# Encoder of a vision tower on one core: the last softmax pair is normalised on VectorE, the last value gather runs on ScalarE, a reciprocal and some transpositions are moved

## The reference, cut to what matters

```python
for l in range(6):
    keys = concat([zeros, x])                      # one zero key ahead of the 37 tokens
    q, k, v = x @ Wq.T + bq, keys @ Wk.T + bk, keys @ Wv.T + bv     # 16 heads of 16
    attn = softmax(where(valid, q k^T / 4, -inf))  # over 38 keys
    o = (attn @ v) @ Wo[l].T + bo[l]
    x = LN(x + o) * ln1_g[l] + ln1_b[l]
    ff = gelu(x @ W1[l].T + b1[l]) @ W2[l].T + b2[l]
    x = LN(x + ff) * ln2_g[l] + ln2_b[l]
```

## Time and profile before

| what | value |
|---|---|
| median of 3 runs | 843.77 us (841.07 to 846.59) |
| span of the profiled execution | 838.5 us |
| encoder phases in it | from about 325 to about 778 us |
| PE busy | 786.8 us, 94% |
| DVE, ACT, POOL busy | 638.9, 458.5, 257.7 us |
| lone phase, PE | 325.1 to 354.0 us |
| a phase A, a phase B | about 36.2 us, about 35.1 us |

### The profile page before, as it was taken

One profiled execution on the slowest core, in us unless ns is written; L12 is line 12 of the kernel. 1 busy time (PEld: TensorE's weight loads), 2 busy tenths in 40 slices (PEclk: granted clock), 3 DMA queues, 4 the chain that ended last, 5 costly groups with the idle time before them and its releaser, 6 DMA issues.

```text
span 838.5 us, 15975 instructions
## 1 busy us (share of the span) xinstructions
PE 786.8 (94%) x5736; PEld 727.0 (87%) x5736; DVE 638.9 (76%) x1285; ACT 458.5 (55%) x820; POOL 257.7 (31%) x297
## 2 busy tenths in 40 slices
PE   5889899999999999799999999999999999979698
PEld 4788669999999998699989989998998999968466
DVE  5696493888877876778797887878788787875686
ACT  3386313433333336576676777677677767735421
POOL 0002100311111100364365146336525524723232
PEclk9899799999999999899999999999999999999999
DMA  5000935989898822010210021021011002200001
GB/s 185 1 1 1 379 105 200 335 298 346 306 336 317 332 75 105 0 40 14 79 61 0 16 97 38 13 100 38 13 50 54 33 13 100 81 23 1 0 1 30
DMA packets 18288, 88.33 MB, mean 105 GB/s; under 512 B 3120, under 2 KB 7472, under 8 KB 12240
## 3 DMA queue, kind: packets, MB, share of 16 engines
q1 hardware_dynamic: 18256, 87.90, 29.5%
HBM read 85.05 MB, written 2.84 MB: 105 GB/s over the span
## 4 chain that ended last, share of the span: by engine, by line
PE 47%; issue 22%; POOL 16%; DVE 11%; ACT 3%; DMA 1%; POOLq 0%; SPq 0%; DVEq 0%; ACTq 0%
PE bank L1093 14%; PE bank L1130 5%; POOL W_L L1925 5%; POOL HF_L L1979 4%; POOL arena L1911 4%; PE bank L1235 3%; POOL WQKV_L L1925 2%; PE bank L1139 2%; PE bank L724 2%; PE bank L866 2%; PE bank L849 2%; PE bank L781 2%; DVE OB L2091 2%; PE bank L766 2%; PE bank L1425 2%
## 5 line engine op out<-in xcount | busy, mean ns | idle before, releaser
L1093 PE MATMUL bank<-arena 128*128 (+1 forms) x1024 | 118.0, 274 | 0.5 <-ACT arena L1669 0.5
L1093 PEld LDWEIGHTS bank<-arena 128*128 128x128 f32 x1024 | 117.4, 192 | 0.7 <-ACT arena L1669 0.7
L1911 POOL TENSOR_TENSOR arena<-arena,srec 111x456 f32<-111x456 f32 x56 | 52.3, 962 | 128.3 <-DVE srec L2079 128.3
L1925 POOL TENSOR_TENSOR W_L<-LW,W_H 128x256 fp32r<-128x256 f32 x96 | 71.0, 778 | 29.5 <-DVE XHL L2520 25.8
L1979 POOL TENSOR_TENSOR HF_L<-arena,HF_H 128x296 fp32r<-128x296 f32 x48 | 43.8, 936 | 86.4 <-ACT HF_H L1826 86.4
L766 PE MATMUL bank<-XHL,W_H 128*128 128x296 f32 x288 | 66.3, 308 | 1.2 <-DVE arena L2068 1.2
L1826 ACT ACTIVATE arena<-bank,vec 128x296 f32<-128x296 f32 x96 | 48.8, 509 | 25.8 <-PE bank L766 17.9
L1937 POOL TENSOR_TENSOR QW<-QW,arena x14 | 22.4, 1599 | 119.0 <-DVE QW L2421 65.6
L1279 PE MATMUL bank<-HF_L,W_H 128*128 128x296 f32 x192 | 57.4, 299 | 0.0
L1279 PE MATMUL bank<-HF_H,W_H 128*128 128x296 f32 x192 | 57.4, 299 | 0.0
L1279 PE MATMUL bank<-HF_H,W_L 128*128 128x296 f32 x192 | 57.4, 299 | 0.0
(11 more groups left out here) (268 smaller groups left out, 2175.6 us busy)
## 6 DMA issues: line engine op xcount, KB each, us to landing
arena<-ew_in SPq DMA_DIRECT2D x16, 2048.0 KB, 8.9
arena<-ew_in SPq DMA_DIRECT2D x16, 1024.0 KB, 6.3
LW<-lw_in SPq DMA_DIRECT2D x12, 1024.0 KB, 4.9
arena<-route SPq DMA_DIRECT2D x32, 185.0 KB, 3.4
LW<-lw_in SPq DMA_DIRECT2D x6, 768.0 KB, 4.3
fp_weights<-arena SPq DMA_DIRECT2D x1, 2048.0 KB, 6.4
arena<-fp_weights SPq DMA_DIRECT2D x1, 2048.0 KB, 7.2
arena<-patches_in SPq DMA_DIRECT2D x2, 864.0 KB, 7.7
```

Of the source, the lines that this page charges most:

```text
L1093: last = mm(o[:, m * CAP:(m + 1) * CAP], w[:, kc, mi * P:(mi + 1) * P], xg(kc, e), start=(kc == 0), stop=(kc == C - 1))
L1911: nc.gpsimd.tensor_tensor(v, v, srec[0:QROWS, s:s + 2, :].unsqueeze(3).to_broadcast([QROWS, 2, C * JH, KEYS]), ALU.mult).then_inc(p_ready, 1)
L1925: last = nc.gpsimd.tensor_tensor(low[:, cols], value[:, cols], high[:, cols], ALU.subtract)
```

## The change

Four things are done in the encoder:

1. **Normalisation.** POOL normalises three pairs of a phase instead of four (`POOL_PAIRS = 3`). DVE multiplies the fourth pair itself (`normalise_last`), in phases A and B between the two residual additions of L2672, in the lone phase after its last reciprocal.
2. **Gather.** DVE gathers three chunks of four (`DVE_GROUPS = 3`). ACT gathers the last (`gather_last`), behind `ln_root` and ahead of `high_weights` and `high_stream`. In the third chunk DVE now takes the reciprocal of the deviation between the second and the third copy. `project_out` waits for DVE's third chunk ahead of its first products and for ACT's chunk ahead of those on feature chunk 1. A copy of the value bias (`vbias`) is made in `set_kbias`.
3. **Transpositions.** In phases A and B, the first of the four jobs of `turn_v` goes ahead of `ln_var_of`.
4. **Lone phase.** Pairs are interleaved: maximum, shift, sum and reciprocal of the early pairs come before those of the late ones on DVE, the exponent of pair 3 comes behind `probs_out` of pair 0 on ACT, and PE transposes two pairs, computes their values, then transposes the other two and computes theirs.

```diff
@@ phase_order
-    att("t", 0, 1, 2, 3)
-    att("o", 0, 1, 2, 3)
+    if y is None:
+        for g in range(2):
+            att("t", 2 * g, 2 * g + 1)
+            att("o", 2 * g, 2 * g + 1)
+    else:
+        att("t", 0, 1, 2, 3)
+        att("o", 0, 1, 2, 3)
@@ TensorE
+                if x and y:
+                    turn_v(rx, plan, hx, (0,))
                 if y:
                     ln_var_of((ly, 0), hy, ones_d)
...
-                    turn_v(rx, plan, hx)
+                    turn_v(rx, plan, hx, (1, 2, 3) if y else range(4))
...
+                elif x:
+                    for g in range(2):
+                        for i in range(2):
+                            transpose_probs(rx, plan, p0 + 2 * g + i)
+                        values(rx, plan, 2 * hx + g)
@@ ScalarE
+            def gather_last(r, plan, h):
+                c = C - 1
+                act.wait_ge(filled["o"], nth("o", 4 * h + 3, r))
+                o = bank_of(plan, ("o", 4 * h + 3))
+                def take(s, lo, hi):
+                    dst = images(OB[lo:hi, h, c, :])[:, 4:8, :]
+                    src = o[lo:hi, 0:4 * QROWS].rearrange("p (b s q) -> p b s q", b=4, s=JH)[:, :, s, :]
+                    return f(dst, src, ACT.Identity, bias=vbias[lo:hi, c:c + 1])
+                take(1, 0, 96).then_inc(o_lead_act, 1)
+                take(2, 96, P)
+                act.wait_ge(o_lead_act, once_a_phase(h, r))
+                take(0, 0, 48).then_inc(o_ready_act, 1)
...
                 if y:
                     ln_square((ly, 1), hy)
                     ln_root((ly, 1), hy)
+                if x:
+                    gather_last(rx, plan, hx)
                 if x:
                     if late_split(x) and late_split(x)[0] == "w1":
                         high_weights(*late_split(x))
@@ ScalarE, lone phase
+                    for i in range(3):
+                        exponent(rx, p0 + i)
+                    probs_out(rx, plan, p0)
+                    exponent(rx, p0 + 3)
+                    for i in range(1, HB // 2):
+                        probs_out(rx, plan, p0 + i)
+                    high_stream(1, 2)
@@ GpSimd
-                    normalise((x[1] * 2 + (x[0] + 2)) * (HB // 2), HB // 2)
+                    normalise((x[1] * 2 + (x[0] + 2)) * (HB // 2), POOL_PAIRS)
@@ VectorE
+            def normalise_last(r, h):
+                p = HB // 2 * (h + 1) - 1
+                dve.wait_ge(s_rec, nth("s", p, r))
+                v.tensor_tensor(pair_probs(p), pair_probs(p), pair_view(srec, p).unsqueeze(2).to_broadcast(
+                    [QROWS, 2 * C * JH, KEYS]), ALU.mult).then_inc(p_ready_dve, 1)
...
                         v.scalar_tensor_tensor(R[:, hy, c, :], bank_of(plan, ("f2", 2 * hy + c))[:, 0:NHALF],
                                                resid[:, ly, C + c:C + c + 1], XD[:, hy, c, :], ALU.add, ALU.add
                                                ).then_inc(ffn_added, 1)
+                        if x and c == 0:
+                            normalise_last(rx, hx)
...
-                if x and y:
-                    gather_values(rx, plan, 2 * hx + 1, lambda c: lv(lx, "bqkv", 2 * C + c), (0,))
-                if y:
+                if x:
+                    gather_values(rx, plan, 2 * hx + 1, lambda c: lv(lx, "bqkv", 2 * C + c), (0,),
+                                  (lambda: ln_recip((ly, 1), hy)) if y else None)
+                else:
                     ln_recip((ly, 1), hy)
-                if x:
-                    gather_values(rx, plan, 2 * hx + 1, lambda c: lv(lx, "bqkv", 2 * C + c),
-                                  (1,) if y else range(C))
```

91 lines of the change are left out of this document (64 added, 27 removed).

## The result

The changed kernel takes 851.01 us (849.49 to 853.56, 6 runs) against 843.12 for the kernel before (841.07 to 846.59, 6 runs) in the same job: ratio 1.0098, interval 1.007 to 1.0125. Measured once more (e13), it takes 849.18 us against 842.91, ratio 1.0072, interval 1.0049 to 1.0095. The change makes the kernel some 6 to 8 us slower; the forecast was 1.75.

The account below looks back on a forecast made before the run. PE, busy 94% of the span, was taken to bound the kernel. Terms 0 + 1.35 - 2.2 - 1.1 - 1.8 + 5.5 = +1.75 us on the 838.5 span gave 840.2, plus 5.3 to the median: 845.5, range 838 to 851.

Parts of the forecast that it names:

- The ScalarE queue behind the gather: Phases B: `gather_last` ahead of `W1_H` makes `XH` late by 1.1 us for the next phase; cost 5.5 in five phases.
- Normalising on DVE: Tail of each phase: DVE multiplies pair 3, so L707 comes 0.1 us earlier; gain 1.1 in eleven phases.
- The reciprocal inside the third chunk: Value gather: the reciprocal ends earlier and L733's wait goes; 0.3 us a phase, gain 1.8 in six phases A.
- The transposition ahead of the variance: Head of each phase: one `turn_v` job fills PE's 0.22 us wait before L724; gain 2.2 in ten phases.
- The lone phase: First transposition 2.0 us sooner, values ending where they did, clock falling as before; taken as 0, bounds 3 gained, 2.5 lost.
- half clock in the whole lone phase: Rival: values cost 0.21 us a record to the end of the lone phase; +2.5, 848.0 us; chance 0.10.
- The first A: First phase A: high weights behind ScalarE's gather delay `values_out`, squares and L724; cost 1.35 us, bounds 0.9 and 2.1.
- order free: Rival: ScalarE's order costs nothing, L781 shows no wait on `XH` in phases B; 834.0 us; chance 0.15.
- port costs more: Rival: `normalise_last` is held by POOL's pair 2 or holds it in full; 848.0 us, up to 853.5; chance 0.17.
- nothing: Rival: PE's waits only change owner and ACT's work is covered; 843.8 us; chance 0.10.

Follow-up runs that it names:

- e13: The changed kernel measured and profiled again, nothing edited: 849.18 us against 842.91 for the kernel before, ratio 1.0072.
- e6: The changed kernel with GpSimd (POOL) normalising all four pairs again, everything else as changed: 852.63 us, ratio 1.0109 to the kernel before.
- e4: The changed kernel with all four `turn_v` jobs back behind the variance: 853.61 us, ratio 1.011 to the kernel before.
- e8: Changed kernel with edits of e2 and e3, lone high weights ahead of ScalarE's gather, second half of keys ahead of root, VectorE order matched: 844.95 us, ratio 1.0043.
- e5: The changed kernel with 29 idle products (17, 6 and 6) added on TensorE in the lone phase: 845.63 us, ratio 1.004 to the kernel before.
- e12: e10 with `high_stream` ahead of `gather_last`, and in the lone phase two chunks gathered before `low_stream(1, 2)` and `W1_H` before ScalarE's gather: 851.58 us, ratio 1.0118.
- e2: The changed kernel with the lone phase in the old order, VectorE's normalisation and ScalarE's gather kept: 849.45 us, ratio 1.0064 to the kernel before.
- e3: The changed kernel with `high_stream` ahead of the high part of W1 on ScalarE in phases B, behind the gather: 844.80 us, ratio 1.0005 to the kernel before.
- e1: The kernel before plus the change's copy of the value bias and three unused semaphores, none of its orders: 842.78 us, ratio 0.9997.
- e9: The kernel before with idle products in its lone phase (17 ahead of the first transposition, 3 and 3 behind pairs): 847.05 us, ratio 1.0062.
- e10: e5 with 8 and 42 more idle products at two places behind the encoder: 843.82 us, ratio 1.0022 to the kernel before.
- e15: The kernel before with the 8 and 42 idle products of e10 behind its encoder, nothing else: 843.64 us, ratio 1.0001.
- e14: e12 with `high_stream` between ScalarE's gather and the weights, as in e3: 837.25 us against 842.91 for the kernel before, ratio 0.9919.

## Why the prediction was wrong, point by point

**The ScalarE queue behind the gather (+5.5): right.** The wait of L802 on `XH` of about 1 us, five times, was forecast (4.9 in 5). The phases B lose 0.9 each against a forecast of 0.78. A term was undersized: the gather cost 0.379 per copy (`Identity` with a bias from SBUF) and not the 0.286 that I took from L1570 in the earlier trace rows, so 1.18 in all instead of 0.87.

```profile
L1625 ACT ACTIVATE OB<-bank,vbias x36: 377/379/381, 358.9 to 757.8; 96x148 f32<-96x148 f32 x12, 32x148 f32<-32x148 f32 x12, 48x148 f32<-48x148 f32 x12
```

**Normalising on DVE (-1.1): right in the sum, wrong in a reading.** Forecast 0.1 a phase, measured 0.12 to 0.13 (e6). The multiplication took 0.74, not 0.63, and `RSUM` was in time, as forecast. POOL's three pairs take 3.17, which is 0.4 more than three of the 0.92 each in the earlier trace rows; the forecast was 0.42. All of it is in the third:

```profile
424.32 1.34 POOL L1974 TENSOR_TENSOR arena<-arena,srec 111x456 f32<-111x456 f32 x1
```

The prediction held it against the skill's rule that POOL's block had grown by only 0.26, less than VectorE's whole instruction. But an instruction can lose only what is left of the other when it is issued. The third pair starts at 424.32, VectorE's multiplication ends at 424.85, so 0.53 was left, and the pair grew by 0.39. On the other side, in the kernel before, `RSUM` started at 416.63 with 0.79 left of a POOL pair and grew by 0.65 (1.11 against 0.466). Both lose what was left, less 0.14. All 55 meetings of `RSUM`, `W_L` and the pairs with the other engine in the profiles of the two kernels come out at what was left less 0.12 to 0.17. With that, the rule of the Trainium skill ("SBUF — State Buffer", Who interferes with whom), that the one that issues first has the shared ports for its whole instruction and the other fully blocks, agrees with the trace on both sides, to 0.17 us.

**The reciprocal inside the third chunk (-1.8): wrong in what it brings.** L754 has no wait left. But a phase A of the loop won 0.12 in all (36.33 to 36.21), e6 gives back 0.10 to 0.12 of that by the normalisation alone, and e4 puts the transposition at 0. So the reciprocal brought next to nothing of the 0.3 in the phases A of the loop; in the second phase A L899 starts 0.29 earlier into the phase than the kernel before's L866 did, and the next phase's second product only 0.20. The wait that was taken away did not set the end of the phase. Only the last A won more (1.6), and no run separates there what did it.

**The transposition ahead of the variance (-2.2): wrong.** The step that failed is "The 0.22 us is a wait", and with it the claim that nothing else sets the scores. By e4 the move is worth 0 in the loop. I had looked at the one engine that released L724 and not at what follows on ScalarE: the root, and behind it `keys(1)`, for which the scores wait. In the kernel before, the scores already began 0.18 us after the keys ended (432.35 + 1.58 = 433.93, scores at 434.11). The job ahead of the variance delays the root, the keys and thus the scores by as much as it had won. The forecast put no price on that chain; e8 shows that turning it round costs 0.66 in each phase A. The four later A's inside the loop won 0.12 each instead of 0.62. Of the 1.6 that the last A won, 0.7 is the shorter wait for `RSUM` behind it (1.3 instead of 2.0); the rest is not taken apart.

**The lone phase (0): wrong, and the largest miss.** The step that failed is "I expect the clock to fall as before ... I take 0". The phase took +3.5 in the first profile and +1.8 in the second. The forecast's events were right to the first values: first transposition 15.4 us into the phase (measured 15.5), first values 18.9 (18.6). Two things behind them were not:

- *The clock.* In the first profile it fell for 13.7 us (349.2 to 362.9) instead of 6.8 before (342.5 to 349.3). The values cost 0.23 us a record to the end, and the output projection ran at half speed as well. This was the rival *half clock in the whole lone phase*: its price of 2.5 for the values is close (7.49 against 5.10), but the projection's (3.82 against 2.24) was missing in it. In e13 the clock was low for 6.8 us, as before. e5 shows that the clock is the larger part: more work on PE, less time (28.3).
- *VectorE's queue ahead of the gather.* The sum had no term for the projection's wait. At full clock it waits 2.48 us for VectorE's third chunk (e13, e5), against 0.62 before; at half clock PE is slow enough to hide most of it (0.76). This is most of the 1.8 that remain in e13. e12 bears it out: with two chunks gathered ahead of `low_stream(1, 2)`, and ScalarE's `W1_H` ahead of its gather, this wait falls from 2.47 to 0.87 and the lone phase from 28.7 to 26.8.

The rival had been given 0.10. The trace of before showed PE idle for 4.4 us just ahead of the fall, and the new order has three waits in a row there (2.31, 1.25, 0.68). That these waits keep the clock low is a guess from one order; that idle products in them bring it back is shown by e5.

**The first A (+1.35, less 0.4): wrong, too dear.** It took 35.9 in both profiles of the changed kernel, 0.2 less than before. L745 came 6.06 into the phase against 5.84 before, not 1.4 late. The weights did run behind the gather, but the lone phase had grown behind that gather by more: PE began the first A 4.2 us after ScalarE's gather started (358.94 to 363.10), where the forecast had 2.5. So the cost lies in the lone phase. In e2, where only 2.1 us lie between the two, it shows (+0.83). The +0.6 to +0.7 of e3, e4 and e6 is another thing: there the clock is at 0.50 for the first 1.8 us of that phase.

**Behind the encoder (no term): missing.** 1.9 us came in a stretch in which nothing was changed. e1 and e9 hold the same instructions there and took 89.0 and 90.8 us, at 0.94 and 0.90. Of eleven kernels without idle products there, nine took 90.6 to 91.4: all that carry the change in whole or in part, and e9, which does not. Why a kernel falls on the one side or the other stays open, and so does whether the change makes the longer one likelier. e10 (88.8 with 50 products more) shows that the clock is the cause of the 2 us; e15 shows that filling a wait there does not always keep it.

The other rivals: *order free* is refuted by the waits of L802, *port costs more* by e6, *nothing* by the phases B. The first median (851.01) ends on the upper edge of the range, the second (849.18) within it; the sum itself was short by 4 to 6 us. Against the first profile the terms missed by: lone phase 3.5, behind the encoder 1.9, later phases A 1.0, phases B 0.7, first A -1.2. What it lacked was the clock as a price of its own at each place where PE stands short of work, and VectorE's queue ahead of the lone projection.

## What to carry to other kernels

On an engine that is busy half the time the order still sets the end: ask for each instruction put into its queue what stands behind it, and put what the next stage needs ahead of what it does not (gather, stream, weights: 6.9 us between two orders that differ by one move). Before a short wait is called won, follow each of the chains that end at the next wait, not only the one that the profile names. Where the pacing engine stands idle several times within some microseconds, price the half clock that may follow over all that runs after it; a few idle products can be cheaper than the wait. They are no sure gain: in e9 they left the lone phase as long as it was, and the kernel was 5 us slower in stretches that they do not touch.

## What the runs showed of the hardware

- Adding instructions to TensorE shortened a phase: with 29 idle products the lone phase took 28.3 us instead of 32.4 and 30.7. With 79 of them and two orders mended (e14) the kernel takes 837.25 us.
- The same kernel falls to the granted clock of 0.50 in somewhat different places from one execution to the next. The changed kernel took 68.3 us for lone + A at a mean clock of 0.88 and 66.6 at 0.92, with the phases of the loop alike. One profile of a stage with a clock below 1.00 is no measure of a change in that stage. The phases of the loop, at 1.00, repeated within 0.05 us in the kernels that share their code.
- Where a VectorE instruction with both sources in SBUF and a GpSimd one meet, the later one loses what is left of the earlier one, less about 0.15 us. `RSUM` takes 0.47 alone, 0.59 with 0.27 left of a GpSimd multiplication, 1.01 with 0.69 left, 1.11 with 0.79 left. A GpSimd multiplication takes 0.95 alone and 1.34 with 0.53 left of VectorE's.
- ScalarE's copy of 148 columns took 0.379 us as `Identity` with a bias per partition, 0.286 as the copy of L1570.
